# Splitting the second half's token tiles one per head over eight heads, behind the exponentials, instead of two per head ahead of them

## The reference

```
HQ, HKV, HD = (32, 8, 64)
q = (x @ Wq.T).reshape(B, L, HQ, HD);  k, v likewise with HKV heads
q = _rope(q);  k = _rope(k)
attn = einsum('bkgqd,bkld->bkgql', qh, kh) * SCALE      # causal mask
p = softmax(attn, axis=-1)
out = einsum('bkgql,bkld->bkgqd', p, vh)
return out @ Wo.T
```

## Time and profile before

| | us |
|---|---|
| median of 3 runs | 1515.1 (1514.55 to 1515.18) |
| the profiled execution, in all | 1515.95 |
| its span | 1514.2 |
| PE busy | 1305.8 (86%) |
| DVE busy | 1074.8 (71%) |
| ACT busy | 924.6 (61%) |
| POOL busy | 588.4 (39%) |
| the 512 exponentials of line 473 | 284.9 busy, mean 558 ns |
| the 8 late xT_lo subtractions | between 496.6 and 547.6 us of the span |

### The profile page before, as it was taken

How to read it: one execution, slowest core, us unless ns; L and a number is a source line. 1 busy time by engine, 2 the same in 40 slices (tenths; PEclk the granted TensorE clock), 3 DMA queues, 4 the chain that set the end, 5 groups by cost and what they waited for, 6 DMA issues and landing times. The chain is left out here.

```text
span 1514.2 us, 26311 instructions
## 1 busy us (share of the span) xinstructions
PE 1305.8 (86%) x7105; PEld 1088.2 (72%) x7112; DVE 1074.8 (71%) x2572; ACT 924.6 (61%) x2177; POOL 588.4 (39%) x476
## 2 busy tenths in 40 slices
PE   2799999999999889999999999997524497899986
PEld 2688888888888778888888888886413375677775
DVE  3588888888888888888888888887746757744312
ACT  2567777677776667767677676776156273555422
POOL 3334444344443334444344443441013052544443
PEclk9899999999999999999999999999655699999998
DMA  4421222212222122222212222111234111011000
GB/s 166 124 72 50 63 62 76 63 49 62 62 77 64 50 84 78 65 65 80 55 49 62 66 80 56 49 45 41 117 116 177 42 42 42 1 42 42 1 28 28
DMA packets 53532, 98.23 MB, mean 65 GB/s; under 512 B 11600, under 2 KB 13648, under 8 KB 51408
## 3 DMA queue, kind: packets, MB, share of 16 engines
q1 hardware_dynamic: 53456, 97.31, 21.9%
HBM read 51.13 MB, written 4.19 MB: 37 GB/s over the span
## 5 line engine op out<-in xcount | busy, mean ns | idle before, releaser
L473 ACT ACTIVATE probs<-probs,neg_max 128x128 f32<-128x128 f32 (+3 forms) x512 | 284.9, 558 | 172.6 <-DVE neg_max L605 172.3
L679 DVE TENSOR_TENSOR pT_lo<-ps_t,pT_hi 128x512 fp32r<-128x512 f32 (+1 forms) x384 | 221.3, 596 | 86.5 <-ACT pT_hi L481 77.7
L750 PE MATMUL ps_s<-k_st,q_st 128*128 128x256 f32 (+2 forms) x1024 | 229.5, 346 | 3.0 <-DVE neg_max L605 3.0
L605 DVE CUSTOM_DVE_ANT_0 probs<-ps_s,mask 128x128 f32<-128x128 f32 (+3 forms) x512 | 228.3, 482 | 2.0 <-PE ps_s L750 1.2
L795 PE MATMUL ps_t<-ident,probs 128*128 128x128 f32 x1280 | 186.0, 276 | 45.3 <-DVE pT_lo L679 29.2
L795 PEld LDWEIGHTS ps_t<-ident,probs 128*128 128x128 f32 x1280 | 148.2, 141 | 69.4 <-DVE pT_lo L679 37.3
L481 ACT ACTIVATE pT_hi<-ps_t 128x512 fp32r<-128x512 f32 (+1 forms) x384 | 186.2, 519 | 8.2 <-PE ps_t L795 5.1
L394 POOL TENSOR_TENSOR o_lo<-o_sum,o_hi 128x512 fp32r<-128x512 f32 x64 | 82.1, 1283 | 264.5 <-ACT o_hi L495 264.5
L807 PE MATMUL ps_o<-pT_hi,v_st 128*128 128x256 f32 (+2 forms) x512 | 168.0, 339 | 0.0
L1176 POOL TENSOR_TENSOR hid_lo<-hid,hid_hi 128x512 fp32r<-128x512 f32 x64 | 83.7, 1309 | 192.4 <-ACT hid_hi L1423 192.4
L807 PE MATMUL ps_o<-pT_lo,v_st 128*128 128x256 f32 (+2 forms) x512 | 155.6, 326 | 0.0
(11 more groups left out here) (195 smaller groups left out, 2961.7 us busy)
## 6 DMA issues: line engine op xcount, KB each, us to landing
q_st<-q_tmp SPq DMA_DIRECT2D x512, 64.0 KB, 2.0
raw<-in_wq_t SPq DMA_DIRECT2D x32, 256.0 KB, 3.0
k_st<-k_st SPq DMA_DIRECT2D x64, 128.0 KB, 2.3
raw<-in_wo_t SPq DMA_DIRECT2D x32, 256.0 KB, 3.0
y<-in_x_t SPq DMA_DIRECT2D x4, 1024.0 KB, 11.0
raw<-in_wkv_t SPq DMA_DIRECT2D x16, 256.0 KB, 3.5
y<-in_x SPq DMA_DIRECT2D x4, 1024.0 KB, 6.1
w_gu<-in_fside_t SPq DMA_DIRECT2D x4, 1024.0 KB, 4.8
```

Source lines behind the costliest of these rows:

```text
L473: act.activation(probs[:, h % 2, SO[i]:SO[i] + SW[i]], probs[:, h % 2, SO[i]:SO[i] + SW[i]], ACT.Exp, bias=neg_max[:, h % 2, i:i + 1], sca ...
L605: dve.tensor_tensor_reduce(out=probs[:, h % 2, SO[i]:SO[i] + SW[i]], in0=ps_s[:, i % 2, 0:SW[i]], in1=mask[:, L - SW[i]:L], scale=-SCALE, ...
L679: dve.tensor_tensor(pT_lo[:, d, :], ps_t[:, (h + k) % 2, 0:P * w].rearrange("p (w c) -> p w c", c=P), f32(pT_hi[:, d, :]), ALU.subtract).t ...
L750: i = pe.matmul(dst, a, c, start=(j == 0), stop=(j == len(terms) - 1))
```

## The change

`x_later` now gives one tile to each of the eight heads 6.1.2, 6.1.3, 7.0.0 to 7.0.3, 7.1.0 and 7.1.1, where it gave two tiles to each of the four heads 7.0.0, 7.0.1, 7.1.0 and 7.1.1. The call moves within the head: on ScalarE from before the next head's first exponential to behind its fourth, on VectorE from between the third pT_lo and the third maximum to the end of the head.

```diff
         def x_later(g, b, h):
 
-            if is_step(g, HKV - 1) and h < 2:
-                return range(8 + 4 * b + 2 * h, 10 + 4 * b + 2 * h)
-            return []
+            at = {(HKV - 2, 1, 2): 8, (HKV - 2, 1, 3): 9, (HKV - 1, 0, 0): 10, (HKV - 1, 0, 1): 11,
+                  (HKV - 1, 0, 2): 12, (HKV - 1, 0, 3): 13, (HKV - 1, 1, 0): 14, (HKV - 1, 1, 1): 15}
+            return [at[g, b, h]] if isinstance(g, int) and (g, b, h) in at else []
@@ ScalarE, body
-                        for t in x_later(g, b, h):
-                            x_part(t)
                         if more:
                             exp(n + 1, (h + 1) % 2, 0)
                             exp(n + 1, (h + 1) % 2, 1)
...
                         if more:
                             exp(n + 1, (h + 1) % 2, 2)
                             exp(n + 1, (h + 1) % 2, 3)
+                        for t in x_later(g, b, h):
+                            x_part(t)
```

## The result

The changed kernel takes 1519.72 us, the median of 20 runs (1516.47 to 1521.39). The kernel before took 1515.33 in 20 runs beside it (1512.55 to 1517.14). The ratio is 1.0026, 95% interval [1.0019, 1.0033]: slower by 4.4 us, where 1509.8 was forecast. The profiled execution took 1517.95 in all.

A forecast was written before the change was run, and what follows sets the result against it. The prediction took TensorE to bound the attention loop. From the profiled 1515.95 us it took off 10.7 of old stalls, added 5.4 for the new places, giving 1510.65, then 0.85 lower for the median: 1509.8, range 1506.6 to 1512.8.

The forecast's parts named there:

- The step that failed: VectorE subtractions meeting GpSimd: each waits out the one running instruction, then takes 0.56 us; prologue's worst case was 1.73 us.
- tile 10: Head 7.0.0: subtraction inside GpSimd's o_lo, pT_lo 0.7 us late, projection covers TensorE, later exponentials slip; 0.3 us.
- tile 14: Head 7.1.0: ScalarE's activation delays k_st and the rotations, hence the last two exponentials; 0.7 us, between 0 and 1.0.
- The old stalls: Nine heads from 6.1.3: the old split costs 10.7 us beyond work done anyway, and all of it goes.
- Tiles 8, 9, 12, 13: Heads 6.1.2, 6.1.3, 7.0.2, 7.0.3: 1.5 us each for 8 and 12, 0 each for 9 and 13, in idle gaps.
- The race: Tiles 8 and 12: GpSimd's k_tmp starts 0.08 us ahead of VectorE, costing 1.5 us each; 0.4 if VectorE came first.
- Tile 11: Head 7.0.1: delayed r_rep copy meets GpSimd's second q_tmp subtraction, so TensorE's transposes start late; 1.2 us, between 0.9 and 1.9.
- Rival (c): All eight subtractions meet running GpSimd instructions with no slack behind: 8 x 1.73 = 13.8 us paid, 1518.2, slower; chance 0.04.
- Rival (a): Nearly all new delay hidden in TensorE's existing waits, some 2 us left over: 1506.4 us; chance 0.12.
- Rival (b): Stalls come back elsewhere through late pT_lo, 1.1 us per tile, 8.8 left: 1513.2 us, no change; chance 0.10.
- Rival (d): Three new TensorE stalls over 1 us each bring back the low clock, 3 x 1.5 = 4.5 us: 1514.3, no change; chance 0.04.
- The forecast's own test for being wrong: Subtractions behind rope_k of 0.68 us, TensorE exponential waits over 1.5 us at 7.0.2 or 7.1.2, or step 7 clock below 1.00.

The follow-up runs named there:

- e1_place_only: Changed kernel with the old division, two tiles per head in 7.0.0, 7.0.1, 7.1.0 and 7.1.1, all at the head's end: 1518.80 us, ratio 1.0016.
- e3_short_gpsimd: Changed kernel with GpSimd's instructions of step 7 cut to 8 of their 512 columns, every order and wait kept: 1507.19 us, one run.
- e7_between_products: Changed kernel with tiles 10 and 14 subtracted between rope_q's two odd multiplications: 1513.22 us, ratio 0.9975 to the kernel before.
- e5_no_h0: Changed kernel with heads 7.0.0 and 7.1.0 emptied: tile 10 moved to 6.1.3, tile 14 to 7.1.1; 1509.27 us, ratio 0.9953.
- e6_idle_places: Changed kernel with late tiles only in h = 1 and h = 3 heads (6.1.1, 6.1.3, 7.0.1, 7.0.3, 7.1.1): 1505.33 us, ratio 0.9936.
- The probes: Two separate kernels computing no layer: VectorE subtractions against five GpSimd ones, varying chaining, request time or an awaited event; all 128 let in at the first boundary.
- e2_spread_only: Kernel before with only the new division, one tile in each of eight heads, in the old place ahead of the exponentials: 1511.93 us, ratio 0.9978.

## Why the prediction was wrong

Its working, tile by tile, against the changed kernel. Measured is the length of the head in which the tile stands less that of an undisturbed head of the same kind, from the reciprocals.

| tile | 8 | 9 | 10 | 11 | 12 | 13 | 14 | 15 | sum |
|---|---|---|---|---|---|---|---|---|---|
| forecast | 1.5 | 0 | 0.3 | 1.2 | 1.5 | 0 | 0.7 | 0.2 | 5.4 |
| measured | 1.6 | -0.1 | 5.1 | 1.1 | 2.0 | -0.1 | 5.8 | 0.1 | 15.5 |

**The step that failed** is "So a subtraction that meets a running GpSimd instruction waits it out and then takes 0.56 us", as used for tile 10: "The subtraction would start at 574.7, inside GpSimd's o_lo, which runs until 575.57", and "It ends at 576.3". The 0.56 us was right in every case. What it waits out was wrong. The rule was taken from the prologue's k_tmp at 35.03 us, which stands alone on GpSimd, and used for a place where four more GpSimd instructions follow o_lo without a gap. That could be seen in the kernel before, one line below the row of o_lo that the prediction took from step 8. Timeline of GpSimd before:

```profile
575.53 1.30 POOL L378 TENSOR_TENSOR q_tmp<-q_tmp 128x512 f32<-128x512 f32 x1
```

The rows of tiles 10 and 11 before, which did stand in a run, seemed to bear the rule out; they were of the kind that is let in. The two tiles account for 10.9 - 1.0 = 9.9 of the 10.1 us by which the sum is off, and those for the distance of 1509.8 from 1519.7. e1_place_only shows the hold to be of the place, e3_short_gpsimd to need GpSimd's work, e7_between_products to grow and shrink with the run, and e5_no_h0 that without it the kernel takes about the forecast's time. The second term that failed hangs on the first: the sum put the lower clock at nothing ("a clock of 1.00 throughout"), and it followed the two long waits.

For tile 14 the prediction looked at ScalarE's activation and the late k_st, and set 0.7 for the exponentials behind them. VectorE's own subtraction was not examined there at all.

**The old stalls.** That the 10.7 us go away was right: no wait for an exponential is left in step 7.

**Tiles 8, 9, 12, 13.** The race fell as forecast: GpSimd's k_tmp started 0.08 us ahead (486.25 and 486.33), the subtraction took 1.76 us and ended at 488.09, 0.56 behind it, and TensorE waited 1.30. Tiles 9 and 13 found their gaps. Tile 12's wait was 1.30 too; the 0.5 us by which its head is above the forecast was not traced.

**Tile 11** has the forecast's size but not, here, its cause. Tile 10's hold had delayed everything by then, so GpSimd's q_tmp pair was over at 514.65, ahead of the r_rep copy at 515.48, and the subtraction took 0.68 us. Part of the head's 1.1 us falls into the stretch at the lower clock, until 516.0. Not all of it need come from there: in e3_short_gpsimd, at clock 1.00, this head is still 0.5 longer than undisturbed. The meeting that the prediction described, the copy inside the second q_tmp subtraction, is what e5_no_h0 and e6_idle_places show: the copy took 1.43 and 1.41 us and the head 1.5 us more, or 1.1 with the head ahead of it, which was 0.5 shorter.

**Rival (c)** had the sign, slower, but wanted every tile to pay 1.73 us; six of eight paid 2.0 or less and two paid over 5. That its 13.8 us came nearest to the 15.5 measured is luck. **Rival (a)** is what e6_idle_places reaches with other heads, not this change. **Rival (b)** had the stalls return elsewhere, at 1.1 us a tile; they returned in two places. **Rival (d)** was right about long waits and wrong about which: behind the two waits of 1.30 us the transposes ran at full speed, behind 4.36 and 4.47 at half. Its price of 1.5 us for each was too low here: step 7 has 65.8 - 60.8 = 5.0 us more of work than step 8. Of this 0.5 to 0.8 also stands in e3, e5 and e6 at a clock of 1.00, so some 4.2 to 4.5 us are left for the two, an estimate. The forecast's own test for being wrong, a clock below 1.00 in step 7, was met. The failed step set off both terms, the 8.8 us of waiting and the slow work behind it; by this reckoning the change would have been about as fast as before without the clock, since the idle time of the step grew by only 0.9. One slip of the prediction changes nothing: its range begins at "(a)'s 1506.6", where (a) is worked out as 1506.4.

## What to carry to other kernels

Before moving a VectorE instruction that reads two operands from SBUF, look at what GpSimd has queued back to back from that moment on, not only at what it is running, and price the move twice: let in at the next boundary, and held up to the end of that run. Put such work where GpSimd is idle: the same eight splits cost 15.5, 10.9 or 3.1 us, by where they stand. Look at the copies beside it too. And where TensorE is the bound, add to a wait of several us the work at the lower clock behind it: at most 1.1 us behind the 4.61 us of the kernel before (61.9 - 60.8), by the estimate above about 2.2 behind each of the changed kernel's two.

## What the runs showed of the hardware that was not expected

- A VectorE subtraction with both inputs in SBUF was held for up to 6.8 us by a run of GpSimd instructions (6.80 in e1_place_only; 6.31 across five in the changed kernel, the one that it met among them), while GpSimd's instructions kept their 1.25 to 1.29 us. The Trainium skill, "SBUF — State Buffer", section "Who interferes with whom", has the shared pair of ports held for one whole instruction. The probes agree with that: the subtraction came in at the next boundary each time. The runs of tiles 10 and 14 don't.
- Where VectorE is let in, both pay: its subtraction ends 0.55 us behind the GpSimd instruction, and GpSimd's next takes 1.71 us instead of 1.26. The r_rep copy ends 0.28 us behind it.
- The clock behind a wait of TensorE. After 1.30 and 2.32 us the transposes ran at full speed. e7_between_products had 2.87 us and a window at 0.83, e2_spread_only 3.10 and 0.84. The kernel before had 4.61 us and 0.83. The changed kernel had 4.36 and 4.47 us and windows at 0.68 and 0.70. So the clock does not follow the length of the wait alone. Window of e7_between_products behind its wait of 2.87 us, which ended at 542.23:

```profile
539.20:549.20 10.00, 7.13 (x37) 5.76 (x36) 7.99 (x19) 6.33 (x18) 6.00 (x5) 0.83 0.59 172
```
